# Linear attention on one core: decay sums as two fp16 passes, a shorter low-rank projection, and position totals as a fifth column group

## The reference

```python
# linear attention, per token: a log decay g for each of the 256 key features
g_logits = x @ Wgk1.T @ Wgk2.T + bgk2          # rank 32
g = log_sigmoid(g_logits) / 32.0
bc = cumsum(g, over the tokens)                # decay sums
o = (q*exp(bc)) against (k*exp(-bc)), causal, applied to v, plus the carried state
o = o * rsqrt(mean(o*o) + EPS) * rms_w
x = x + (o * silu(x @ Wg.T)) @ Wout.T

# mixture of experts, routing
scores = sigmoid(x @ router_w.T)
mask = one_hot(top_2(scores + bias))           # tokens are then placed expert by expert
```

## Time and profile before

| | us |
|---|---|
| median of 3 runs | 1641.43 (1640.24 to 1641.56) |
| span of the profiled execution | 1643.4 |
| TensorE busy in it | 1604.4 (98%) |
| VectorE busy | 1180.6 (72%) |
| ScalarE busy | 875.8 (53%) |
| GpSimd busy | 706.3 (43%) |

### The profile page before, as it was taken

The page is one execution under the profiler, slowest core; times in us unless marked ns, Lnnn a source line. Parts: engine busy times, 40 slices in busy tenths (PEclk is TensorE's granted clock), DMA queues, the critical chain, the costliest instruction groups (busy, mean ns, idle before and its releaser), DMA issues.

```text
span 1643.4 us, 42424 instructions
## 1 busy us (share of the span) xinstructions
PE 1604.4 (98%) x15094; PEld 1081.8 (66%) x15095; DVE 1180.6 (72%) x2536; ACT 875.8 (53%) x1510; POOL 706.3 (43%) x660
## 2 busy tenths in 40 slices
PE   7999999999999999999999999999999999998998
PEld 3665566666666777766555666666657777777576
DVE  7677775666666666668865556666688878888886
ACT  5354543444366666664333334444376666675664
POOL 2442242444235445442332333434245567777343
PEclk9999999999999999999999999999999999999999
DMA  7132233333311211003210123333422033131001
GB/s 263 52 103 87 88 103 91 109 110 111 88 39 27 36 28 26 0 1 101 91 40 26 39 79 103 110 111 103 107 64 51 2 79 80 55 67 42 22 30 52
DMA packets 91303, 115.71 MB, mean 70 GB/s; under 512 B 9424, under 2 KB 76528, under 8 KB 91184
## 3 DMA queue, kind: packets, MB, share of 16 engines
q1 hardware_dynamic: 70832, 71.17, 15.3%
q0 software_dynamic: 20352, 42.88, 9.1%
HBM read 66.11 MB, written 47.90 MB: 69 GB/s over the span
## 4 chain that ended last, share of the span: by engine, by line
PE 81%; DVE 7%; ACT 5%; issue 3%; POOL 2%; DMA 1%; SPq 0%; another core or an unknown queue 0%; DVEq 0%; ACTq 0%; POOLq 0%
PE ps L1968 18%; PE ps L1970 18%; PE ps L1969 18%; PE ps L2261 3%; PE ps L2260 3%; PE ps L2210 3%; PE ps L2211 3%; PE ps L1984 2%; PE ps L2182 2%; PE ps L2163 2%; PE ps L2360 1%; PE ps L2498 1%; PE ps L2532 1%; PE ps L2510 1%; POOL expert_x L753 1%
## 5 line engine op out<-in xcount | busy, mean ns | idle before, releaser
L781 POOL DMA_INDIRECT routed<-work x142 | 136.2, 959 | 237.5 <-DVE work L1641 232.4
L1968 PE MATMUL ps<-later_hi,work 128*128 (+1 forms) x632 | 202.6, 321 | 0.4 <-DVE work L1621 0.2
L1970 PE MATMUL ps<-later_hi,work 128*128 (+1 forms) x632 | 202.5, 320 | 0.0
L1969 PE MATMUL ps<-later_lo,work 128*128 (+1 forms) x632 | 202.5, 320 | 0.0
L1968 PE MATMUL ps<-xt_hi,wsh 128*128 128x512 f16 x508 | 192.6, 379 | 2.6 <-DVE work L1512 2.2
L1970 PE MATMUL ps<-xt_hi,wsh 128*128 128x512 f16 x508 | 192.5, 379 | 0.0
L1969 PE MATMUL ps<-xt_lo,wsh 128*128 128x512 f16 x508 | 192.5, 379 | 0.0
L952 ACT ACTIVATE work<-ps 128x512 f32<-128x512 f32 x128 | 76.4, 597 | 171.8 <-PE ps L1970 162.8
L1968 PE MATMUL ps<-wsh,work 128*128 128x256 f16 x512 | 139.5, 273 | 0.7 <-DVE work L1441 0.6
L1969 PE MATMUL ps<-wsh,work 128*128 128x256 f16 x512 | 139.5, 273 | 0.2 <-issue 0.2
L1970 PE MATMUL ps<-wsh,work 128*128 128x256 f16 x512 | 139.5, 273 | 0.0
(11 more groups left out here) (267 smaller groups left out, 4306.4 us busy)
## 6 DMA issues: line engine op xcount, KB each, us to landing
work<-expert_x SPq DMA_DIRECT2D x142, 129.0 KB
yg<-in_w_later SPq DMA_DIRECT2D x9, 496.0 KB
w1q<-in_w_later SPq DMA_DIRECT2D x9, 496.0 KB
yg<-in_w SPq DMA_DIRECT2D x16, 256.0 KB
values<-wsh SPq DMA_DIRECT2D x8, 512.0 KB, 3.9
later_hi<-values SPq DMA_DIRECT2D x16, 256.0 KB, 4.7
later_lo<-values SPq DMA_DIRECT2D x16, 256.0 KB, 4.9
out_x<-x SPq DMA_DIRECT2D x8, 512.0 KB, 3.0
```

What stands on the lines that cost most here:

```text
L781: nc.gpsimd.indirect_dma_start(routed[:, :], bass.IndirectOffsetOnAxis(m.homes[:, i:i + 1], 0), m.t_y[:, i % 4, :], None).then_inc(s[f"til ...
L1968: nc.tensor.matmul(out_, a[0], b[0], start=start, stop=False)
L1969: nc.tensor.matmul(out_, a[0], b[1], start=False, stop=False)
L1970: return nc.tensor.matmul(out_, a[1], b[0], start=False, stop=stop)
```

## The change

The low-rank weights get a fourth copy. ScalarE overwrites the upper half of the fourth copy with the lower half of Wgk1 (new function `low_rank_weights`, in ScalarE's program at the start of the last expert sequence; the copy for Wgk2, formerly L1127, moves there too). One 128-row matmul then gives x upper by both halves; a 96-row matmul adds x lower. The logits matmul sums over 128 rows instead of 96.

The decay is made in two instructions, split by ScalarE (`upper_decay`) and GpSimd (`lower_decay`) into fp16 halves that lie in the space of `m.soft`, and summed by two fp16 matmuls for each block, against a new fp16 copy of `cumref`. The totals of `positions` become columns 32 to 39 of the same accumulation. The two semaphores for scaled q and k become one. The chunks grow from 992 to 996 columns.

```diff
+                def lower_decay(g):                       # GpSimd
+                    for j in range(2):
+                        pool.wait_ge(s["g_hi"], g * 2 + j + 1)
+                        nc.gpsimd.tensor_tensor(m.g_lo[j], m.lb[:, 2 * j:2 * j + 2], m.g_hi[j], ALU.subtract).then_inc(s["g_lo"], 1)
...
                     if not is_last(g):
+                        lower_decay(g + 1)
                         rstd_of(g + N0(n) + 2)
...
                 second_rows(n - 1, 2)
+                lower_decay(0)
                 lower_values(0)
...
+                def upper_decay(g):                       # ScalarE
+                    for j in range(2):
+                        act.wait_ge(s["g_ready"], g * 2 + j + 1)
+                        nc.scalar.activation(m.g_hi[j], m.lb[:, 2 * j:2 * j + 2], ACT.Copy).then_inc(s["g_hi"], 1)
...
                         nc.scalar.activation(flat(m.squares[:, j]), ...
+                        if j == 0 and not is_last(g):
+                            upper_decay(g + 1)
...
                 keys(0)
+                upper_decay(0)
                 queries(0)
...
-                    nc.vector.scalar_tensor_tensor(out=m.lb, in0=m.lb, scalar=0.0, in1=m.soft, op0=ALU.min,
-                                                   op1=ALU.subtract).then_inc(s["g_ready"], 1)
+                    for j in range(2):
+                        own = slice(2 * j, 2 * j + 2)
+                        nc.vector.scalar_tensor_tensor(out=m.lb[:, own], in0=m.lb[:, own], scalar=0.0, in1=m.soft[:, own], op0=ALU.min,
+                                                       op1=ALU.subtract).then_inc(s["g_ready"], 1)
...
+                pe.wait_ge(halves_set, 4)                 # low_rank
+                own = [gk1[0][:, k * 4 * LOW:(k + 1) * 4 * LOW] for k in range(KT)]
+                nc.tensor.matmul(ps[:, bank, :], own[0], xt(u, 0)[0], start=True, stop=False)
                 for k in range(KT):
-                    ins = mm3(ps[0:3 * LOW, bank, :], both(gk1, slice(k * 3 * LOW, (k + 1) * 3 * LOW)), xt(u, k), k == 0, k == KT - 1)
+                    nc.tensor.matmul(ps[0:3 * LOW, bank, :], own[k][:, 0:3 * LOW], xt(u, k)[1], start=False, stop=False,
+                                     skip_group_check=True)
+                ins = nc.tensor.matmul(ps[:, bank, :], own[1], xt(u, 1)[0], start=False, stop=True)
...
-                    for t in range(TPS - 1):              # positions
-                        nc.tensor.matmul(pos[:, (t + 1) * NE:].rearrange("p (t e) -> p t e", e=NE), ones16,
-                                         m.mask[:, t:t + 1].broadcast_to([P, TPS - 1 - t, NE]), start=False, stop=(t == TPS - 2),
-                                         skip_group_check=True)
                     for t in range(TPS):
-                        ins = nc.tensor.matmul(total, ones16, m.mask[:, t], start=(t == 0), stop=(t == TPS - 1),
+                        ins = nc.tensor.matmul(pos[:, (t + 1) * NE:].rearrange("p (t e) -> p t e", e=NE), ones16,
+                                               m.mask[:, t:t + 1].broadcast_to([P, TPS - t, NE]), start=False, stop=(t == TPS - 1),
...
-                    pe.wait_ge(s["g_ready"], g + 1)       # cums
-                    for p in range(GPAIR):
-                        for c in range(TPS):
-                            ins = nc.tensor.matmul(ps[:, GCUM[p], c * P:(c + 1) * P], m.lb[:, c, p * P:(p + 1) * P], const("cumref"),
-                                                   start=True, stop=True)
+                    for j in range(2):
+                        pe.wait_ge(s["g_lo"], g * 2 + j + 1)
+                        for c in range(2):
+                            for p in range(GPAIR):
+                                out_ = ps[:, GCUM[p], (2 * j + c) * P:(2 * j + c + 1) * P]
+                                own = slice(p * P, (p + 1) * P)
+                                nc.tensor.matmul(out_, m.g_hi[j][:, c, own], cumref16[:], start=True, stop=False)
+                                ins = nc.tensor.matmul(out_, m.g_lo[j][:, c, own], cumref16[:], start=False, stop=True)
```

More of the change, by code:

```diff
@@ L120, in build @@
         causal16, ones_col = sb("causal16", [P, P], F16), sb("ones16", [P, 2], F16)
+        cumref16 = sb("cumref16", [P, P], F16)
         ones16 = ones_col[:, 0:1].broadcast_to([P, P])
@@ L428, in gla_space @@
             m.gate = at([2, 2, 2, GPAIR, DV])
+            m.g_hi, m.g_lo = ([m.soft[:, 2 * j + n].bitcast(F16).rearrange("p (c d) -> p c d", c=2) for j in range(2)] for n in range(2))
             m.up, m.down = r([GPAIR, SEQ]), r([GPAIR, SEQ])
@@ L931, in low_rank_hi, with low_rank_weights @@
                 act.wait_ge(S[n]["t_ready"], g + 1)
-                nc.scalar.activation(t[0:3 * LOW], ps[0:3 * LOW, bank, :], ACT.Copy, scale=1 / WS).then_inc(S[n]["t_hi"], 1)
+                nc.scalar.activation(t, ps[:, bank, :], ACT.Copy, scale=1 / WS).then_inc(S[n]["t_hi"], 1)
+            def low_rank_weights():
+                act.wait_ge(w_lo_done, len(PIECES) + CHUNKS + 1)
+                first = [w.rearrange("p (k c) -> p k c", k=KT)[:, :, 3 * LOW:4 * LOW] for w in gk1]
+                nc.scalar.activation(first[0], first[1], ACT.Copy).then_inc(halves_set, 1)
+                second = [w[2 * LOW:3 * LOW, :] for w in gk2]
+                nc.scalar.activation(second[0], second[1], ACT.Copy).then_inc(halves_set, 1)
             def ffn0(n):
@@ L946, in body @@
                         act.wait_ge(w_lo_done, len(PIECES))
+                    if is_last(g) and ahead_of_gla(n):
+                        low_rank_weights()
                     if not is_first(g) and not is_last(g) and not is_second(g):
@@ L1125, in body @@
                         exp_and_ln()
-                nc.scalar.activation(gk2[0][2 * LOW:3 * LOW, :], gk2[1][2 * LOW:3 * LOW, :], ACT.Copy).then_inc(halves_set, 1)
                 exp_and_ln()
@@ L1257, in _ @@
             nc.scalar.activation(ones_col[:], const("ones")[:, 0:2], ACT.Copy).then_inc(halves_set, 1)
+            nc.scalar.activation(cumref16[:], const("cumref"), ACT.Copy).then_inc(halves_set, 1)
             xt_hi_of(0, 0)
@@ L2052, in positions @@
                     pe.wait_ge(s["mask_ready"], (g + G0) + 1)
-                    pos, total = ps[:, 0, 64:64 + TPS * NE], ps[:, 0, 96:96 + NE]
-                    nc.tensor.matmul(pos, causal16[:], m.mask.rearrange("p t e -> p (t e)"), start=True, stop=False,
+                    pos = ps[:, 0, 64:64 + (TPS + 1) * NE]
+                    nc.tensor.matmul(pos[:, 0:TPS * NE], causal16[:], m.mask.rearrange("p t e -> p (t e)"), start=True, stop=False,
                                      skip_group_check=True)
-                    for t in range(TPS - 1):
-                        nc.tensor.matmul(pos[:, (t + 1) * NE:].rearrange("p (t e) -> p t e", e=NE), ones16,
-                                         m.mask[:, t:t + 1].broadcast_to([P, TPS - 1 - t, NE]), start=False, stop=(t == TPS - 2),
-                                         skip_group_check=True)
                     for t in range(TPS):
-                        ins = nc.tensor.matmul(total, ones16, m.mask[:, t], start=(t == 0), stop=(t == TPS - 1),
+                        ins = nc.tensor.matmul(pos[:, (t + 1) * NE:].rearrange("p (t e) -> p t e", e=NE), ones16,
+                                               m.mask[:, t:t + 1].broadcast_to([P, TPS - t, NE]), start=False, stop=(t == TPS - 1),
                                                skip_group_check=True)
@@ L2288, in logits @@
                             sl = slice((2 * j + t) * P, (2 * j + t + 1) * P)
-                            ins = nc.tensor.matmul(ps[:, banks[j], t * H * DK:(t + 1) * H * DK], t_[0:3 * LOW, sl], gk2[0][:, :],
+                            ins = nc.tensor.matmul(ps[:, banks[j], t * H * DK:(t + 1) * H * DK], t_[:, sl], gk2[0][:, :],
                                                    start=True, stop=True)
```

26 lines of the change are left out of this document (13 added, 13 removed).

## The result

The changed kernel takes 1632.06 us (median of 4 runs, 1631.86 to 1632.93) where the kernel before takes 1641.43: a ratio of 0.9942 with an interval of 0.9930 to 0.9953, so 9.4 us or 0.57% less. The forecast was 1633.7 in a range of 1631.8 to 1638.4. In a later series the same kernel had 1633.52 against 1642.43, ratio 0.9948 (0.9936 to 0.9960).

A forecast was written before the change was run, and what follows sets the result against it. TensorE, busy throughout the attention's middle bodies, was taken as the bound. Terms: -2.6 projection, -5.7 sums, -1.0 positions, +0.9 new wait, +0.7 prologue, -7.7 us together: 1633.7 us, range 1631.8 to 1638.4.

The forecast's parts named there:

- projection, bodies 1 to 6: Low-rank projection on TensorE: four passes instead of six save 0.43 us in each of bodies 1 to 6, 2.6 us.
- sums, 7 bodies: Decay sums on TensorE: 16 fp16 matmuls at 0.060 us take 0.97 instead of 1.78 us, 5.7 us less over 7 bodies.
- new wait, bodies 1 to 5: TensorE's decay sums: GpSimd's second lower half arrives almost as wanted; 0.1 us lost per body for an unhidden weight load.
- new wait, body 0: Decay sums of body 0: GpSimd's second half ends near 489.0, TensorE wants it at 488.75; 0.4 us lost.
- prologue: First decay sums, ahead of body 0: they wait for GpSimd's halves and end 0.7 us later, all reaching body 0.
- positions: Position matmuls on TensorE: three fewer save 0.075 us at each of 16 places, 1.2 us, taken as 1.0.
- the 34.7 to 34.9: Expected distance in us between decay sums in the middle bodies, where it was 35.9 before the change.
- (c): Rival, decay sums: each of 16 matmuls waits 98 ns for its weights; only 3.5 us gained, 1637.9 us; chance 0.06.
- (a): Rival, new wait: GpSimd's lower half takes about 1.6 us, not 1.16, eating the gain; 1641 us; chance 0.15.
- (b): Rival, slower: GpSimd's lower half takes 2.3 us, so the kernel loses 4.5 us; 1646 us; chance 0.05.
- (d): Rival, cheaper: GpSimd isn't held or starts ahead of `combine`, and passes go at 0.056 us; 1632.4 us; chance 0.10.
- The carry to the median: Terms were summed against the profiled span, 1643.4 us, and carried to the median of 1641.43, which lies 2.0 lower.

The follow-up runs named there:

- the two prologue experiments: Changed kernel with the prologue's decay sums in float32 as before: 1631.62 us; that kernel with the first values' halves also made in two parts: 1630.99 us.
- the second profile of before: The kernel before the change, unchanged, profiled again: a span of 1639.8 us.

## Why the prediction was right, and where it missed

The prediction stands: the direction, the mechanism and the size, 7.7 us forecast and 9.4 measured. The measured 1632.06 lies near the lower end of its range, 1631.8; 1.2 of the 1.7 us between forecast and measurement are terms of the attention in the table below, and the rest lies in stages that move by a us from run to run. By its steps:

| step | forecast | measured |
|---|---|---|
| projection, bodies 1 to 6 | -2.6 | -2.60 |
| sums, 7 bodies | -5.7 (0.81 each) | -6.2 (0.89 each) |
| new wait, bodies 1 to 5 | +0.5 | 0.0 |
| new wait, body 0 | +0.4 | +0.3 |
| prologue | +0.7 | +0.6 |
| attention | -6.7 | -7.94 |
| positions | -1.0 | -1.2 on TensorE, of which the second expert stage shows 0.46; beside the sums 1 to 3 more elsewhere |

*Sums.* The 0.060 a matmul came from 24 of them with the first and last edge of the group in it. Between two starts in the middle of such a stream there are 0.056, and the sixteen go at that. That term was mis-sized by 0.5 us over seven bodies. With the 0.1 us of the next point it is why the sums stand 34.58 us apart, below the 34.7 to 34.9 that the forecast set as its sign. The 98 ns of a weight load never showed, so (c) fell. The 81 ns of the Trainium skill ("TensorE: Matmul & The Clock Gate", "Back-to-back issue gap") would have given an estimated 1636.0; the trace has 0.056 us for such a stream.

*The new wait in bodies 1 to 5.* The working had the halves end at 560.5 and TensorE want the second at 560.56. The trace has the same in its own time: an end 0.1 us ahead of the start, 0.04 of it slack. Lock and price of GpSimd were right (3.09 for the two, where 3.1 follows from the forecast's 557.36 to 560.5). The step that failed is the 0.1 us a body that was added for a weight load that can't be hidden: it isn't paid while the operand arrives in time. That is 0.5 us of the miss.

*Body 0 and prologue.* 0.29 of the 0.4 forecast, and 0.56 more in the prologue for 0.7, for the reason given. That the loss reaches body 0 whole is shown by the two prologue experiments.

*The rivals.* (a) and (b) rest on a longer lower half; its price was 1.16 us (in the median of sixteen), and only `combine` made one longer. With 1.04 us of added work ahead of each half the kernel is slower than before, so (b) was no straw man: the change runs with 0.04 us to spare. (d) has the right total, 1632.4, for a half wrong reason: the passes do go at 0.056, but GpSimd is held, as the forecast had it.

*The carry to the median.* The sum was set against the span of a long execution and carried over by its distance to the median, 2.0 us. But a time lies about 2 us above the span of its own execution (1641.82 and 1639.8 for the second profile of before), so that execution was some 4 us longer than the median one. That was harmless, since the gain lies in the attention, which repeats to 0.03 us.

*Positions.* Right where the three matmuls stand: 0.075 us at each of 16 places. Not foreseen is what the program's other stages do when it changes elsewhere: 1 to 3 us, up to a third of the gain. Which way that goes was luck.

## What to carry to other kernels

A stream of fp16 matmuls costs its spacing in mid-stream (0.056 us for 128 columns here), and two such passes beat one float32 pass (0.22) only as long as the engine that makes the lower half delivers in time; so set the price of that engine's work, and of the lock that holds it, against the moment at which TensorE wants the result, body by body. Before a gain of half a per cent is read from two spans, cut them into stages at an instruction that comes once a sequence: stages that repeat to hundredths carry the argument, stages that move by a us from run to run don't. A part that is measured alone can show less than in company, when it also shifts what lies behind it; here a change of a few instructions moved the places at which TensorE waits for its program.

## What the runs showed of the hardware

GpSimd's subtraction of float32 into fp16 keeps to one line over all sizes seen: 64 columns 0.30 us, 448 1.03, 512 1.16, 1024 2.13 and 2048 4.07, so 0.19 us and 1.89 ns a column (one form of 1024 columns, `xn` less its upper half, takes 2.07). Its record begins when it is issued, also where it is held by VectorE; its length then holds the wait.

TensorE stood for up to 1.3 us in the windowed attention and at the start of the stage behind it for nothing that the views name, in groups of small matmuls or right behind them, in some kernels and not in others with the same work there. One such group of the changed kernel:

```profile
1345.67 1.16 PE L2531 MATMUL ps<-work,wsh 32*64 32x64 f32 x64
```

These are 64 records in 1.16 us, 0.018 each, and with their weight loads the densest stream of instructions that was seen. The traces show that the stands are late instructions. The page lists a DMA queue that loads instructions (q8), with 84 packets before and 83 after, of 16384 bytes each. In the fourteen profiles TensorE has 33 stands of 0.19 to 1.26 us with no releaser, and each of them ends 1.26 to 1.74 us behind the landing of a packet of that queue, though these packets come only every 3 to 10 us there. In each profile they lie a multiple of 256 of TensorE's records apart, its sequencer's included, to within one: in the first profile of the changed kernel they are ahead of records 22652, 23676 and 30075. Other stands of this kernel and of the variants that leave the length of TensorE's program as it is come at 26491 and 30331, again multiples of 256 away. So TensorE stood there for its next block of instructions. The Trainium skill, "Runtime: NRT & Kernel Launch", section "Instruction fetch mechanics", holds that fetching is hidden by the rate of issue; these stands are an exception.

The eight profiles with the positions' part have 83 packets, the six without it 84, so this part moves the places at which the blocks begin. That fits what it takes away beside the sums; no run moved these places alone, so the 1 to 3 us are put down to them by this argument only.
